# Fourteen gather tiles a layer instead of seven fetched row by row from SyncE, with wider, aligned register loads

## The reference

```
edge_index = stack([src, dst])
h = relu(layernorm(x)); x = x + L0(h)   # mean of h @ W over in-edges and itself, + b
h = relu(layernorm(x)); x = x + L1(h)   # lap = segment_sum(h[src] * edge_weight, dst)
                                        # leaky_relu((h+lap)@W1 + b1 + (h*lap)@W2 + b2), rows normalised
h = relu(layernorm(x)); x = x + L2(h)   # m = (h @ Wn.T + bn)[src] * ef,  ef = two-layer softplus net of edge_attr
                                        # agg = segment_sum(m, dst); two-layer softplus net of agg
h = relu(layernorm(x)); x = x + L3(h)   # GAT, 4 heads: softmax over in-edges of leaky_relu(a_src[src] + a_dst[dst]),
                                        # weighted sum of h[src] @ W, layernorm, relu, + h
```

## Time and profile before

| | us |
|---|---|
| median of 3 runs | 5119.45 (5119.01 to 5122.34) |
| profiled execution, first to last instruction (span) | 4118.2 |
| median less span | 1001.25 |
| POOL busy | 2981.3 (72% of the span) |
| DVE busy | 2593.0 (63%) |
| PE busy | 2408.9 (58%) |
| ACT busy | 1816.6 (44%) |

### The profile page before, as it was taken

One profiled execution on the slowest core, in us unless ns is written; L12 is line 12 of the kernel. 1 busy time (PEld: TensorE's weight loads), 2 busy tenths in 40 slices (PEclk: granted clock), 3 DMA queues, 4 the chain that ended last, 5 costly groups with the idle time before them and its releaser, 6 DMA issues. The chain is left out here.

```text
span 4118.2 us, 65293 instructions
## 1 busy us (share of the span) xinstructions
PE 2408.9 (58%) x13340; PEld 2021.0 (49%) x13340; DVE 2593.0 (63%) x7266; ACT 1816.6 (44%) x4202; POOL 2981.3 (72%) x3172
## 2 busy tenths in 40 slices
PE   3666666655566666656544444444566666666667
PEld 2555555554454555546434334443554555454556
DVE  5444444443566666667644444444669999999997
ACT  3444444422243444432211111111457887788886
POOL 4777777776777777777677777777757777777763
PEclk8787777777677787877765666656779999999899
DMA  7444444432344443432333333333466222222221
GB/s 148 125 116 126 116 126 116 126 83 69 94 116 125 116 124 115 126 106 67 100 110 105 110 105 105 110 105 109 115 117 124 58 57 58 57 57 57 57 53 32
DMA packets 242878, 405.96 MB, mean 99 GB/s; under 512 B 68322, under 2 KB 141691, under 8 KB 242492
## 3 DMA queue, kind: packets, MB, share of 16 engines
q0 software_dynamic: 99456, 206.27, 20.8%
q10 hardware_dynamic: 69920, 120.96, 10.4%
q1 hardware_dynamic: 73116, 74.56, 6.2%
HBM read 331.90 MB, written 67.79 MB: 97 GB/s over the span
## 5 line engine op out<-in xcount | busy, mean ns | idle before, releaser
L756 POOL DMA_INDIRECT t_work<-d_T,t_tabG x3100 | 2928.1, 945 | 1038.5 <-issue 848.1
L1657 PE MATMUL ps<-t_work,t_acc 128*128 x2592 | 463.0, 340 | 439.7 <-POOLq L723 396.5
L1657 PEld LDWEIGHTS ps<-t_work,t_acc 128*128 128x128 f32 x2592 | 414.9, 245 | 516.9 <-issue 516.6
L1730 DVE TENSOR_TENSOR t_acc<-t_acc,ps 128x128 f32 (+1 forms) x732 | 210.3, 287 | 513.6 <-PE ps L594 209.5
L1832 ACT COPY ps<-t_acc 128x512 f32 x244 | 140.6, 588 | 779.1 <-POOLq L723 777.1
L1719 DVE TENSOR_TENSOR t_hT<-t_work,ps 128x512 f32<-128x512 f32 x244 | 167.2, 685 | 503.0 <-ACT ps L1832 502.9
L1657 PE MATMUL ps<-t_hT,t_acc 128*128 128x128 f32 x1296 | 264.0, 388 | 272.2 <-DVE t_acc L1730 263.4
L1657 PEld LDWEIGHTS ps<-t_hT,t_acc 128*128 128x128 f32 x1296 | 249.1, 295 | 288.9 <-DVE t_hT L1719 285.0
L1657 PE MATMUL ps<-t_work 128*128 x1312 | 239.9, 347 | 249.7 <-POOLq L723 220.2
L627 ACT ACTIVATE t_acc<-ps,t_bcol 128x1024 f32<-128x1024 f32 x98 | 109.1, 1113 | 612.4 <-DVE ps L640 590.5
L2145 PE MATMUL ps<-t_work,t_hT 128*128 x1960 | 316.8, 310 | 100.2 <-DVE t_acc L2155 81.9
(11 more groups left out here) (205 smaller groups left out, 4478.6 us busy)
## 6 DMA issues: line engine op xcount, KB each, us to landing
d_edge_net<-t_acc ACTq DMA_DIRECT2D x98, 512.0 KB
t_acc<-d_edge_net SPq DMA_DIRECT2D x98, 512.0 KB, 4.2
t_work<-d_T,t_tabG POOLq DMA_INDIRECT x3100
t_acc<-in_edge_attrT ACTq DMA_DIRECT2D x96, 512.0 KB, 4.2
t_acc<-d_T SPq DMA_DIRECT2D x1792, 0.5 KB
t_acc<-d_T SPq DMA_DIRECT2D x896, 0.5 KB
t_work<-d_T SPq DMA_DIRECT2D x896, 0.5 KB
t_acc<-d_T ACTq DMA_DIRECT2D x12, 790.1 KB, 17.0
```

Source lines behind the costliest of these rows:

```text
L756: pool.indirect_dma_start(out=work[:, at:at + width], out_offset=None, in_=table, in_offset=bass.IndirectOffsetOnAxis(ap=idx[:, g * QUAD + ...
L1657: last = pe.matmul(sums(layer, s, width), masks[s % MASKS][:, k, :], rows_k, start=(k == 0), stop=(k == QUAD - 1))
L1730: dve.tensor_tensor(out=o, in0=o, in1=sums(layer, s, width), op=ALU.add).then_inc(e_acc[layer], 1)
```

## The change

What it does:

- `SIDE` is 14 and `SIDE_PER` is 10: SP fetches fourteen tiles a layer, ten rows per group, over about 13 groups each; POOL issues 768 gathers a layer and not 775.
- `SIDE_REGS` = 32: the source offsets are loaded 32 registers at a time, where they were loaded five at a time (fewer at a block's end). The buffer that they are loaded from begins at a multiple of four elements, where it began at element 6321 of the partition's row (in layer 3 at 4522).
- The counts that SP waits on are loaded eight at a time and not four, POOL's in layer 3 32 at a time and not 14; `winB`, `slotB` and `needB` eight at a time and not four; ACT's control numbers in layer 2 eight for two steps.
- A count that a semaphore is waited for is first masked by a register operation (`v & 0xfff`), one for each such wait.
- The tables `closing`, `closingB` and `closing2` are computed in scratch and copied to their tiles, two short DVE operations more.

```diff
-SIDE, SIDE_PER, SIDE_READ = 7, 5, 64
+SIDE, SIDE_PER, SIDE_READ, SIDE_REGS = 14, 10, 64, 32
...
+        COUNT = 0xfff
+        def count(v, lo, hi):
+
+            return within(v & COUNT, lo, hi)
...
-        ENDS = 14
+        ENDS = 32
...
-                    pool.wait_ge(used, ends[n - read[0]])
+                    pool.wait_ge(used, count(ends[n - read[0]], 1, top_at))
...
-            row = acc[0:1, NT * ACC3:XC] if layer < 3 else work[0:1, (RING * QUAD + 2) * ROW3:]
-            return row[:, c % 2 * SIDE_READ:(c % 2 + 1) * SIDE_READ].bitcast(I32)
+            held, lo = (acc, -(-NT * ACC3 // 4) * 4) if layer < 3 else (work, -(-(RING * QUAD + 2) * ROW3 // 4) * 4)
+            return held[0:1, lo + c % 2 * SIDE_READ:lo + (c % 2 + 1) * SIDE_READ].bitcast(I32)
...
-            for c in range(SIDE_READS):
-                lo, hi = [min(max(SIDE_PER * m - SIDE_READ * c, 0), SIDE_READ) for m in (n, n + 1)]
-                if lo == hi:
-                    continue
-                if lo == 0:
+            for r in range(SIDE_PER * n, min(SIDE_PER * (n + 1), SIDE * P)):
+                c, at = divmod(r, SIDE_READ)
+                if at == 0:
                     sp.wait_ge(s_src[c % 2], 16 * (SIDE_READS // 2 * layer + c // 2 + 1))
-                found = numbers(ENG.SP, side_sources(layer, c)[:, lo:hi], hi - lo, 0, (N - 1) * row)
-                for r, at in zip(range(c * SIDE_READ + lo, c * SIDE_READ + hi), found):
-                    j, p = divmod(r, P)
-                    sp.dma_start(side_rows(layer, j)[p:p + 1, :].bitcast(U8)[:, 0:row], table_b[:, bass.ds(at, row)])\
-                        .then_inc(s_row[layer][j % 4], 16)
+                if at % SIDE_REGS == 0:
+                    row_from[layer] = numbers(ENG.SP, side_sources(layer, c)[:, at:at + SIDE_REGS], SIDE_REGS, 0, (N - 1) * row)
+                j, p = divmod(r, P)
+                sp.dma_start(side_rows(layer, j)[p:p + 1, :].bitcast(U8)[:, 0:row],
+                             table_b[:, bass.ds(row_from[layer][at % SIDE_REGS], row)]).then_inc(s_row[layer][j % 4], 16)
...
-                if n % 4 == 0:
-                    ends = numbers(ENG.SP, closed_at[0:1, n:n + 4], 4, 1, top_at)
+                if n % 8 == 0:
+                    ends = numbers(ENG.SP, closed_at[0:1, n:min(n + 8, GROUPS)], min(8, GROUPS - n), 1, top_at)
...
-                sp.wait_ge(used, ends[n % 4])
+                sp.wait_ge(used, count(ends[n % 8], 1, top_at))
...
-            if add in range(QUADSB):
-                sums_at[add] = numbers(ENG.DVE, winB[0:1, steps_of(add)], QUAD, 0, (BB - 1) * ACC3)
+            if add in range(0, QUADSB, 2):
+                v = numbers(ENG.DVE, winB[0:1, two_quads(add)], 2 * QUAD, 0, (BB - 1) * ACC3)
+                sums_at[add], sums_at[add + 1] = v[:QUAD], v[QUAD:]
...
-            if head in range(QUADSB) and head % 4 == 0:
-                needs[head // 4] = numbers(ENG.DVE, needB[0:1, head:head + 4], 4, 1, TILES)
+            if head in range(0, QUADSB, 8):
+                needs[head // 8] = [count(v, 1, TILES) for v in numbers(ENG.DVE, needB[0:1, head:head + 8], 8, 1, TILES)]
```

More of the change, by code:

```diff
@@ L44 @@
 SIDE_READS = SIDE * P // SIDE_READ
-assert P % SIDE_READ == 0
+assert P % SIDE_READ == 0 and SIDE_READ % SIDE_REGS == 0 and SIDE_READS % 2 == 0
 assert SIDE_AT[-1] < GROUPS
@@ L675, in numbers @@
             return v
+        COUNT = 0xfff
+        assert TILES <= COUNT and 2 * STEPS <= COUNT
+        def count(v, lo, hi):
+            return within(v & COUNT, lo, hi)
         def within(v, lo, hi):
             return nc.s_assert_within(v, lo, hi, skip_runtime_bounds_check_because="a part of the staircase's row")
-        def control(engine, s):
-            edge, win, off, slot = numbers(engine, ctl[0:1, 4 * s:4 * s + 4], 4, 0, NT * ACC3)
-            return (within(edge, QUAD, TILES), within(win, 0, NT), within(off, 0, (NT - 1) * ACC3),
-                    within(slot, 0, (RING - 1) * PITCH))
         RAW_GROUP = RING // 2
@@ L778, in side_sources @@
         def side_sources(layer, c):
-            row = acc[0:1, NT * ACC3:XC] if layer < 3 else work[0:1, (RING * QUAD + 2) * ROW3:]
-            return row[:, c % 2 * SIDE_READ:(c % 2 + 1) * SIDE_READ].bitcast(I32)
-        assert MLP + 11 * GRP + 2 * ACC3 <= BB * ACC3 and NT * ACC3 + 2 * SIDE_READ <= XC
-        assert (RING * QUAD + 2) * ROW3 + 2 * SIDE_READ <= work.shape[1] and SIDE_READS % 2 == 0
+            held, lo = (acc, -(-NT * ACC3 // 4) * 4) if layer < 3 else (work, -(-(RING * QUAD + 2) * ROW3 // 4) * 4)
+            assert lo + 2 * SIDE_READ <= (XC if layer < 3 else work.shape[1])
+            return held[0:1, lo + c % 2 * SIDE_READ:lo + (c % 2 + 1) * SIDE_READ].bitcast(I32)
+        assert MLP + 11 * GRP + 2 * ACC3 <= BB * ACC3
         def read_sources(layer, c):
@@ L2029, in steps_of, with two_quads @@
             return slice(QUAD * n, QUAD * (n + 1))
+        def two_quads(n):
+            return slice(QUAD * n, QUAD * (n + 2))
         def slots_of(engine, n):
-            return [within(v, 0, (RING * QUAD - 1) * ROW3)
-                    for v in numbers(engine, slotB[0:1, steps_of(n)], QUAD, 0, (RING * QUAD - 1) * ROW3)]
+            v = numbers(engine, slotB[0:1, two_quads(n)], 2 * QUAD, 0, (RING * QUAD - 1) * ROW3)
+            return v[:QUAD], v[QUAD:]
         def meet_step(n):
@@ L2188, in raise_to @@
                 if head in range(QUADSB):
[L2189 removed]
+                    head_step(head, k, rows_of[head], needs[head // 8][head % 8])
             next(links, None)
```

41 lines of the change are left out of this document (25 added, 16 removed).

## The result

| | before | after |
|---|---|---|
| median, us | 5120.9 (5119.01 to 5131.49, 4 runs) | 5460.02 (5449.64 to 5477.34, 4 runs) |
| span of the profiled execution, us | 4118.2 | 5476.0 |
| its own time, us | not given | 5477.34 |

The ratio is 1.0669 (95% interval 1.0641 to 1.0698): 339 us slower, where 42 faster had been forecast.

The account below looks back on a forecast made before the run. POOL issuing gathers back to back at 1.249 us was taken as the bound; 35.0 us for 28 fewer gathers, less 1 of stalls, times 1.243, brought 5119.45 to 5077 us, with 8 of 10 from 5069 to 5102.

Parts of the forecast that it names:

- Gathers, 28 x 1.249 = 35.0 us: POOL, all four layers: seven fewer gathers a layer at 1.249 us each take 35.0 us off the span.
- SP's work sum for layer 2: SP in layer 2: a net 221 us of added work fits into the 321 us that SP waits.
- Layer 3 and DVE's step: Layer 3: SP's announcements come up to 2 us late; DVE's step, between -0.1 and +0.25 us, is taken as unchanged.
- the stalls booked at 1 us: POOL in layer 3: stalls from late announcements, booked as 1 us lost from the 35.0 gained.
- from span to time: Whole run: the 34 us span gain was scaled by 5119.45 / 4118.2 = 1.243, giving 5077 us.
- the cover: SP, all layers: its added work was to fit into time it spends waiting, 320.9 us in layer 2.
- the ring of 39 us: Between SP and POOL: eight groups deep, so SP's lateness of 2 us would not reach POOL in layers 0 to 2.
- The rival "SP becomes the bound": SP: a load of 32 takes more than 3.9 us, SP's waits vanish and the time goes up; chance 0.06.
- The rival of a loss in what lies around the span: Outside the span: it grows with program length, 140 us up against 34 down, 5225 us; chance 0.03.
- the Trainium skill's power profile: Whole run: sequencer and GpSimd software costs read 1.18 to 1.25 times the default's; cited because 1.243 lies in that band.
- 200 ns a register: SP's loads: by this rate a load of 32 takes 6.4 us and the time is above 5550.
- The range: Whole run: 8 of 10 chances lie between 5069 and 5102 us.

Follow-up runs that it names:

- i1: The changed kernel run again, unedited, on a chip without the 0.70 us stops: 4092.9 us against 4123.3 for the kernel before.
- e1: The kernel before plus only the masks on counts waited for, on a chip with the 0.70 us stops: 5138.7 us, ratio 1.0072 to the kernel before.
- e2: The changed kernel with seven side tiles and five rows a group, on a chip with the stops: 5097.9 us, ratio 0.9982 to the kernel before.
- h1: The changed kernel with four side tiles and five rows a group, on a chip with the stops: 5121.2 us, ratio 1.0036 to the kernel before.
- j2: The changed kernel with two side tiles and two rows a group, on a chip with the stops: 5176.5 us, ratio 0.9976 to the kernel before.
- g2: The changed kernel with constant row addresses, without MOVEs and source loads, on a chip with the stops: 5163.5 us, ratio 1.0118 to the kernel before.
- e6: The changed kernel with four side tiles and five rows a group, on a chip without the stops: 4145.2 us, ratio 1.0046 to the kernel before.
- e3: The kernel before plus masks, with fourteen side tiles, ten rows a group and loads the old way, on a chip with the stops: 5707.7 us, ratio 1.1183.

## Why the prediction failed, point by point

- **Gathers, 28 x 1.249 = 35.0 us: right.** 3072 gathers at 944 ns in both profiles of after. Where POOL sets the end, the whole change gave 30.4, and the span of i1 is 4091.6 us where 4084 had been forecast.
- **SP's work sum for layer 2: right for executions of the kind that it was read from.** Forecast were 100 us of waits left less 8.7; i1 has 92.7. The load of 32 took 2.12 us (forecast 2.3, limit 3.9). POOL's waits for SP came to 10.8 us, in pieces of at most 1.0.
- **Layer 3 and DVE's step: right there too.** DVE's wait for SP fell from 31.2 to 3.0 us as its room shrank; the stalls booked at 1 us can't be told from the missing 5.
- **The step that failed is "from span to time".** The 1001.25 us by which the runs exceeded the span were taken for something around the program, or for everything being slower in proportion. They were neither. The profile and the timed runs were executions of two kinds. In the timed kind the instruction streams of SyncE and TensorE stop for 0.70 us a time, and GpSimd waits for them. Its own gathers keep their 0.94 + 0.30 us. The argument "POOL's pace makes up 94% of the span" was made in the one execution to which it applied.
- **With it fell the cover, and with the cover the sign of the result.** SP's 0.33 us a row, its 321 us of waits and the ring of 39 us were true without steps. With them a row takes 0.54 us, and SP has 5.0 us of waits for its consumer in layer 2 of e1 before a row is added. 896 rows a layer are 1792 instructions more for a stream that is stopped again and again: the work went onto the path in place of into idle time, and four layers became 339 us longer. A ring evens out single late groups; it can't make up for a stream whose work per group is on average longer than the group.
- **The rival "SP becomes the bound"** had the right symptom (SP's waits gone, `e_free` waits in POOL) and the wrong cause, a dear load. Its chance of 0.06 was priced by the load alone. The rival of a loss in what lies around the span fell with the thing itself. The sentence on the Trainium skill's power profile (Advanced Engine Details and Errata, Clock Domains) doesn't explain the ratio either: under it all software costs of sequencer and GpSimd would be longer in proportion, but POOL's 944 ns and SP's median MOVE of 29 ns are the same in both kinds of execution. The Trainium skill's 200 ns a register (Runtime: NRT & Kernel Launch, Instruction fetch mechanics) isn't borne out by 2.12 us for 32, 66 ns each. On the same page the Trainium skill describes these as loads from HBM, and the ones here read on-chip memory. The loads that begin elsewhere than at a multiple of 16 bytes take 208 to 302 ns a register (last section).
- **The range** was built on the price of known parts. A gap of 24% between a profile and its own runs was bridged by one multiplication, and had deserved the larger part of the doubt. That the change gains 30.4 us without steps confirms the parts. It doesn't make the forecast for the timed kind a near miss.

What stays open: what makes the steps, and why on some chips only. Shown is that they hit SyncE and TensorE, and ScalarE once its instructions come densely, in moves, transfers, counts and between matmuls, and that no trace of the other kind has any on SyncE, on ScalarE or between TensorE's matmuls. That they come from the way instructions reach the engines would fit, but no run shows it. Nor is it shown what sets the floor of some 5,100 us that e2, h1 and j2 share; in layer 3 of h1 a gather takes 1.66 to 1.71 us even where SyncE has no steps, and POOL waits 251 us for TensorE's line 2161. The matmuls of that line are themselves longer with steps, 422 ns (median in h1, e2 and g2) against 275 (e6, i1). How much of layer 3's time is that and how much TensorE's steps, no run tells.

## What to carry to other kernels

When a profile's span and the measured time differ by more than a few us, they are two different executions: don't scale one to the other, and don't spend idle time that only the profile has. Idle time of a queue is room for instructions only in the regime in which it was measured. A stream of many small instructions (7,168 moves and as many row DMAs here) is the part that suffers first when the stream itself is disturbed, so that replacing few gathers by many small instructions is a bet: 0.6% won on one kind of chip, 6.8% lost on the other. No version tried beats both kernels on both kinds of chip; nearest is e2, the new loads with the old tiles, 0.2% faster with steps (just clear of noise, 0.9965 to 0.9999) and not run without.

## What the runs showed of the hardware

- The same program takes 4093 us on one chip and 5452 on another, with the same median durations of SyncE's moves (29 ns) and transfers (228 ns) and of GpSimd's gathers (944 ns). What differs are stops of 0.70 us and multiples of it between and within instructions, also within a MOVE (29 ns in the median, up to 1408), and longer matmuls in layer 3 (last point).
- A load of 32 registers on SyncE from a place at a multiple of 16 bytes takes 2.12 us (median of 168), 66 ns a register. Where a load begins decides much of its price. The loads of five in the profile of before begin 20 bytes further each time within a block. By the kernel's addresses, counted from the start of the tile's row, the medians are 0.70 us at a multiple of 16 bytes, and 1.08, 1.25 and 1.51 us at 4, 8 and 12 bytes past one (126 loads each, layers 0 to 2). Four successive ones, at 0, 4, 8 and 12 bytes past:

```profile
L671 SPq TENSOR_LOAD <-t_acc x1: 692/692/692, 2112.9 to 2112.9; - x1
L671 SPq TENSOR_LOAD <-t_acc x1: 1074/1074/1074, 2119.5 to 2119.5; - x1
L671 SPq TENSOR_LOAD <-t_acc x1: 1263/1263/1263, 2122.7 to 2122.7; - x1
L671 SPq TENSOR_LOAD <-t_acc x1: 1532/1532/1532, 2127.4 to 2127.4; - x1
```

  Ten registers took 1.11 us at a multiple of 16 bytes and 2.08 at 8 past one in layer 3 of e3, and 2.09 and 2.23 at 4 and 12 past one in its layers 0 to 2. No run reads 32 from such a place, so what the alignment alone brought to the change isn't measured.
- 5,880 semaphore counts on an idle ScalarE cost nothing measurable on the one kind of chip (ratio 1.0054 against 1.0046 for the kernel without them) and some 110 us on the other.
- TensorE's granted clock was 0.60 and 0.72 in layers 2 and 3 of the profile after, where the earlier trace rows has 0.65 and 0.91 and i1 0.65 and 0.92: both are means between the two levels, 1.2 and 2.4 GHz. TensorE was busy 764 of 1380 us in layer 3 of the profile after and 622 of 977 in the earlier trace rows, with no more work done: in the layer that is stretched by stops the granted clock is lower, and line 2161's matmuls take 422 ns in the median and not 275.
